# MoE layer of a small vision tower: the first expert matrix is copied into fixed buffers before use

## Chip, core and metric

The kernel is one program on one core of a Trainium2 chip. Its time is the device time of that core in microseconds (us), as the median of several runs. Five engines work side by side and meet at semaphores: TensorE (PE, matmuls; PEld is its weight load), VectorE (DVE), ScalarE (ACT), GpSimd (POOL) and SyncE (SP, which here only issues DMAs). SBUF is the on-chip memory of 128 partitions; a DMA is carried out by up to 16 DMA engines.

## What is computed

Patches of 32 images (1,152 tokens of width 192) are embedded, pass three steps of a reference attention with layernorms, a softmax attention and then a mixture of experts (MoE). Only the MoE part changes:

```python
logits = xn @ gate_w                                   # 8 experts
top_logits, top_idx = jax.lax.top_k(logits, 2)
top_gates = softmax(top_logits)
h = gelu(einsum('td,edh->teh', xn, w1) + b1)           # w1[e]: 192 x 768
y = einsum('teh,ehd->ted', h, w2) + b2                 # w2[e]: 768 x 192
out = sum over the two chosen experts of gate * y
```

## The kernel before

**Data.** Each token's row is scattered twice by POOL's indirect DMAs into `srt_dram`, sorted by expert and padded so that each expert starts at a tile of 128 rows. There are always 25 tiles (`NTILE`). Which expert a tile belongs to is known only at run time: DVE computes it (`exp_ready`, numbers packed in `packs`) and where its rows start (`row_i`, `place_ready`). Every weight is held twice in SBUF, as a float16 high part and a bfloat16 low part (`w1h`, `w1l`, `w2h`, `w2l`, all 8 experts), which ACT and POOL make from float32 pieces during the attention steps (SP loads a piece of `w1` as 96 x 768, ahead of its turn).

**One tile, i.** SP reads the tile's start from `row_i` and loads 128 x 194 values from `srt_dram` into a ring of eight (`xsrt`, shown as `xT` in the profile, since it lies in that tensor). PE transposes it (`columns_of`, `srtT`), ACT applies the layernorm gain (`srtT_affine`), DVE rounds it to `xh`, POOL takes the rest `xl`. `first(i)` is 12 groups of three matmuls (six blocks of 128 hidden units, two halves of 96 input features, each high x high, high x low, low x high), with the expert's weights as the stationary operand; their address depends on the expert, so each group has register instructions. ACT adds the bias and applies gelu, one instruction for each of the six blocks of 128 x 128. DVE splits the result (`split`), and `second(i)` is 18 matmuls of 192 columns against `w2`. DVE adds `b2`, POOL scatters the rows to `y_dram`.

**Order.** Everything is written out by hand, engine by engine. On PE the order is `columns_of(i+1)`, `first(i)`, `second(i-1)`. SP, in its own queue, waits for `place_ready` and `row_stored` and then issues the 25 row loads; the one for tile i waits until ring slot i-8 is free. After the last tile SP loads `y_dram` back in tiles of 108 tokens (`yab`, the last one 72), PE sums, and a last layernorm stores the output.

Of the kernel before, what the change touches and what calls it, by code (L numbers as in the profile page):

```python
# [5 lines left out]
ALU = mybir.AluOpType  # L6
# [35 lines left out]
RING, YB = 8, 3  # L42
PACK = 7
# [14 lines left out]
def vit_kernel(nc, d, out):  # L58
    with ExitStack() as ctx:
# [13 lines left out]
        vecs = sb("vecs", [T, 5, C])  # L73
# [13 lines left out]
        wqk = sb("wqkh", [HF, 2, 2, 384], F16), sb("wqkl", [HF, 2, 2, 384], BF16)  # L87
# [3 lines left out]
        w1h, w1l = sb("w1h", [HF, EXP, 2, HID], F16), sb("w1l", [HF, EXP, 2, HID], BF16)  # L91
        w2h, w2l = sb("w2h", [P, EXP, HJ, C], F16), sb("w2l", [P, EXP, HJ, C], BF16)
        b1 = sb("b1", [128, EXP, HJ])
# [13 lines left out]
        e1T = sb("e1T", [E1, NTOK])  # L107
# [104 lines left out]
        xh, xl = sb("xh", [HF, 2, 2, P], F16), sb("xl", [HF, 2, 2, P], BF16)  # L212
# [13 lines left out]
        x_in = [sem(f"x_in{t}") for t in range(NT)]  # L226
# [3 lines left out]
        ffn_in = sem("ffn_in")  # L230
        piece_in = [sem(f"piece_in{b}") for b in range(4)]
        srt_in = [sem(f"srt_in{b}") for b in range(RING)]
        y_stored = [sem(f"y_stored{b}") for b in range(YB)]
        yab_in = [sem(f"yab_in{t}") for t in range(NT)]
# [28 lines left out]

        def expert_of(engine, loaded, i):

            if i % PACK == 0:
                loaded[0] = engine.value_load(packs[0:1, i // PACK:i // PACK + 1], min_val=0, max_val=EXP ** PACK - 1)
            return (loaded[0] >> 3 * (i % PACK)) & EXP - 1

        def weights(q, low):  # L270

            if q < 2:
                return wqk[low][:, q].rearrange("p k c -> p (k c)"), stage[q % 4][0:HF, 0:4 * C]
            if q == 2:
                return wvp[low][:].rearrange("p a k c -> p (a k c)"), stage[q % 4][0:HF, 0:4 * C]
            e, k = (q - 3) // 3, q % 3
            if k < 2:
                return (w1h, w1l)[low][:, e, k, :], stage[q % 4][0:HF, 0:HID]
            return (w2h, w2l)[low][:, e].rearrange("p j c -> p (j c)"), stage[q % 4]
# [3 lines left out]
        FFN = ["vbb", "qkbm", "gate", "b1", "route", "rank"]  # L283
        tiles = dict(gains=gains, vbb=vbb, vecs=vecs, fc1=fc1, fc1b=fc1b, fc2=fc2, fc2b=fc2b, ident=ident, sel=sel, rowm=rowm,
                     kw=kw, wqT=wqT, bdm=bdm, wq=wq, wqv=wqv, pairm=pairm, wpa=wpa,
                     qkbm=qkbm, gate=gate, b1=b1, route=route, rank=rank)

        @block.sync
        def _(sp):
            sp.dma_start(tokw[:], d["tokw"]).then_inc(tokw_in, 16)  # L290
            for t in range(2):
                sp.dma_start(xT[:, t], d["xT"][t]).then_inc(x_in[t], 16)
            for name in EARLY:
                sp.dma_start(tiles[name][:], d[name]).then_inc(early_in, 16)
            for t in range(2, NT):
                sp.dma_start(xT[:, t], d["xT"][t]).then_inc(x_in[t], 16)
# [6 lines left out]
            for i in range(NI + 1):  # L303
                if i < NI:
                    sp.wait_ge(S["o_ready"], i + 1)
                    for j in range(JB):
                        sp.dma_start(scratch[i % SCR].rearrange("(j h n d) -> j n h d", j=JB, h=HEADS, n=N)[j],
                                     osb[j * N:(j + 1) * N, i % OB, j].rearrange("p (h d) -> p h d", h=HEADS)
                                     ).then_inc(o_stored[i % 2], 16)
                if 1 <= i <= NI:  # L310
                    q = i - 1
                    sp.wait_ge(o_stored[q % 2], 16 * JB * (q // 2 + 1))
                    if q >= 4:
                        sp.wait_ge(S["ocT_psum"], q - 3)
                    sp.dma_start(oc[:, q % 4], scratch[q % SCR].rearrange("(p c) -> p c", p=T)).then_inc(oc_loaded[q % 4], 16)

                for q in range(PIECES):
                    if (turn_of(q - 4) if q >= 4 else 0) != i:
                        continue
                    if q == 2:  # L320
                        sp.wait_ge(S["e1_psum"], len(CHUNKS))
                        sp.wait_ge(S["k_psum"], 4)
                    if q >= 4:
                        sp.wait_ge(S["low_ready"], q - 3)
                    e, k = q // 3 - 1, q % 3
                    if e < 0:
# [15 lines left out]
            for b in range(YB):  # L342
                sp.wait_ge(y_stored[b], 16 * len(range(b, NTILE, YB)))
            for t in range(NT):
                n = T if t < NT - 1 else LAST
                sp.dma_start(yab[0:n, t].rearrange("p k c -> p (k c)"),
                             y_dram[2 * t * T:2 * (t * T + n)].rearrange("(p k) c -> p (k c)", k=2)).then_inc(yab_in[t], 16)
# [8 lines left out]
        def _(pe):  # L356
# [23 lines left out]
            for t in range(NT + 1):  # L380
                if t == 1:
                    pe.wait_ge(early_in, 16 * len(EARLY))
                if t < NT:
                    pe.wait_ge(x_in[t], 16)
# [141 lines left out]
            for i in range(NT + 6):  # L526
                if i < NT:
# [6 lines left out]
                    for a in range(2):  # L534
                        for g in range(3):
                            cols = slice(g * 128, (g + 1) * 128)
                            last = split_mm(bank[5 + a][:, g * T:(g + 1) * T], [(wqk[0][:, a, k, cols], wqk[1][:, a, k, cols]) for k in range(2)], x)
# [86 lines left out]
            def first(i, e):  # L624

                pe.wait_ge(S["xh_ready"], i + 1)
                pe.wait_ge(S["xl_ready"], i + 1)
                for j in range(HJ):
                    if j % 2 == 0 and hid_turn(i, j) >= 4:
                        pe.wait_ge(S["hid_ready"], 2 * (hid_turn(i, j) - 3))  # L630
# [26 lines left out]
            for i in range(NTILE + 1):  # L657
                if i + 1 < NTILE:
                    columns_of(i + 1)
                if i < NTILE:  # L660
                    e[i % 2] = expert_of(pe, loaded, i)
                    first(i, e[i % 2])
# [9 lines left out]
            pe.wait_ge(S["hid_ready"], HJ * NTILE)  # L672
# [5 lines left out]
            for t in range(NT):  # L678
                n = T if t < NT - 1 else LAST
                pe.wait_ge(yab_in[t], 16)  # L680
# [8 lines left out]
        def _(act):  # L689
# [155 lines left out]
            act.wait_ge(S["exp_ready"], 1)  # L845
            loaded = [None]
            for i in range(NTILE):
                if i + 1 < NTILE:
                    srtT_affine(i + 1)
                e = expert_of(act, loaded, i)  # L850
# [16 lines left out]
        def _(dve):  # L867
# [30 lines left out]
            V.memset(ocT[HF:], 0.0).then_inc(S["pad_ready"], 1)  # L898
            link(V.memset(exp_f[:], 0.0))
# [255 lines left out]
            def sorted_high(i):  # L1155
                dve.wait_ge(S["srtT_ready"], i + 1)
                V.tensor_copy(xh[:, i % 2], x32[:, i % 2]).then_inc(S["xh_ready"], 1)  # L1157

            def split(i):
                for a in range(2):  # L1160
                    cols = slice(a * 3 * P, (a + 1) * 3 * P)
                    o = slice(a * 3, (a + 1) * 3)
                    dve.wait_ge(S["hid_ready"], HJ * i + 3 * (a + 1))
# [38 lines left out]
        def _(pool):  # L1202
# [32 lines left out]
            for i in range(3, NI + 6):  # L1235
                if 5 <= i < NI + 5:
# [15 lines left out]
            for i in range(NT + 6):  # L1252
                if 0 <= i - 4 < NT:
# [24 lines left out]
            def sorted_low(i):  # L1278
# [3 lines left out]
                G.tensor_tensor(xl[:, i % 2], x32[:, i % 2], xh[:, i % 2], ALU.subtract).then_inc(S["xl_ready"], 1)  # L1282
# [97 lines left out]
```

## Time and profile before

| | us |
|---|---|
| median of 3 runs (547.84 to 556.38) | 551.46 |
| the profiled execution: its own time | 549.04 |
| the profiled execution: span from first to last instruction | 547.2 |
| PE busy in it | 445.6 |
| DVE / ACT / POOL busy | 318.5 / 237.0 / 220.9 |
| DMA queue q1 (issued by SP), share of 16 engines | 19.1% |

Busy time is a sum over the span. PE is busy for four fifths of it. The granted TensorE clock averages 0.813 of full speed. "DMA share" in later rows is the busy share of the 16 DMA engines together, so a share of 1 is all 16 at work.

### The profile page before, as it was taken

How to read it: one execution, taken by the hardware profiler on the slowest of the kernel's cores; microseconds unless marked ns; L12 is line 12 of the kernel's file. 1: busy time of each engine (PE TensorE's matmuls, PEld its weight loads, DVE VectorE, ACT ScalarE, POOL GpSimd, SP SyncE). 2: the span in 40 equal slices, each digit the busy share in tenths (PEclk: the TensorE clock that was granted, in tenths of full speed). 3: DMA queues.
4: the chain of work that ended last, by engine and by line, in shares of the span. 5: the costliest groups of instructions: out<-in, count | busy, mean ns of one | idle time of the engine just before them, and what ended most of it. 6: DMA issues, size and time to landing. Idle time of an engine off the chain costs nothing.

```text
span 547.2 us, 13333 instructions
## 1 busy us (share of the span) xinstructions
PE 445.6 (81%) x4370; PEld 352.7 (64%) x4370; DVE 318.5 (58%) x912; ACT 237.0 (43%) x687; POOL 220.9 (40%) x334
## 2 busy tenths in 40 slices
PE   3992588799999965489999998763299999999975
PEld 3972545466666544389898897663287677676764
DVE  1110323388888888687878877545466556565523
ACT  0130324365555532277666654401265554555403
POOL 1000003345545547545446744355334534445214
PEclk9996587799999995567667867555589999999988
DMA  8609513454545541000000000002211111110023
GB/s 265 221 11 323 192 45 74 120 126 108 118 116 122 110 104 18 2 1 3 1 4 14 13 15 14 13 25 85 65 45 46 42 26 41 28 31 21 11 75 121
DMA packets 52161, 38.46 MB, mean 70 GB/s; under 512 B 36187, under 2 KB 45541, under 8 KB 51328
## 3 DMA queue, kind: packets, MB, share of 16 engines
q1 hardware_dynamic: 48832, 26.89, 19.1%
q10 hardware_dynamic: 1008, 7.15, 4.0%
q0 software_dynamic: 2256, 3.57, 2.0%
q8 instruction: 39, 0.64, 0.5%
q14 instruction: 26, 0.21, 0.1%
HBM read 24.00 MB, written 14.33 MB: 70 GB/s over the span
## 4 chain that ended last, share of the span: by engine, by line
PE 61%; DVE 12%; issue 9%; POOL 6%; DMA 4%; ACT 3%; ACTq 3%; SPq 2%; POOLq 0%; DVEq 0%
PE wide L358 29%; PE bank L358 25%; PE bank L363 3%; ACTq L706 3%; PE bank L545 2%; POOL rstd L1222 2%; DVE xs L895 2%; ACT xT L801 2%; POOL srt_dram L1249 1%; PE bank L621 1%; DMA bdm<-in_bdm 1%; DVE rm L985 1%; PE wide L545 1%; DVE xT L993 1%; DMA xT<-in_w 1%
## 5 line engine op out<-in xcount | busy, mean ns | idle before, releaser
L1295 POOL DMA_INDIRECT y_dram<-qkbm,ydst x25 | 25.8, 1032 | 70.7 <-PE bank L358 27.3
L691 ACT ACTIVATE xT<-wide 108x384 f32<-108x384 f32 (+1 forms) x70 | 26.0, 407 | 60.1 <-PE wide L358 44.9
L895 DVE TENSOR_SCALAR xs<-yb,mv,rstd 108x192 f32<-108x192 f32 x24 | 43.5, 1814 | 5.4 <-POOL rstd L1222 5.0
L358 PE MATMUL bank<-xT 108*32 108x96 f32 (+4 forms) x629 | 32.3, 265 | 16.5 <-ACT xT L691 10.7
L358 PEld LDWEIGHTS bank<-xT 108*32 108x32 f32 (+4 forms) x629 | 24.1, 143 | 33.2 <-issue 21.3
L724 ACT ACTIVATE xT<-bank,gains 96x128 f32<-96x128 f32 (+1 forms) x72 | 28.7, 454 | 38.4 <-PE bank L621 31.9
L358 PE MATMUL bank<-wqv,xTs 128*108 128x384 f32 x96 | 41.0, 554 | 3.4 <-DVE xT L993 3.4
L1167 DVE CAST xs<-xT 128x384 f16<-128x384 f32 x50 | 21.6, 431 | 35.7 <-ACT xT L855 34.7
L358 PE MATMUL wide<-w2h,xs 128*128 x300 | 41.9, 248 | 0.4
L1249 POOL DMA_INDIRECT srt_dram<-row,dst x22 | 22.8, 1037 | 42.0 <-DVE dst L1050 34.0
L1221 POOL TENSOR_SCALAR veps<-mv 108x1 f32<-108x1 f32 x46 | 10.7, 232 | 70.8 <-DVE mv L889 70.2
L358 PE MATMUL wide<-xT,wqkh 96*128 96x108 f16 (+1 forms) x264 | 35.1, 287 | 3.3 <-DVE xT L1014 3.3
L358 PE MATMUL bank<-xh,w1h 96*128 96x128 f16 x152 | 35.4, 234 | 2.5 <-DVE xh L1157 1.3
L1244 POOL TENSOR_TENSOR wqkl<-xT,wqkh 96x768 bf16<-96x768 f32 x2 | 3.2, 1634 | 83.9 <-ACT wqkh L691 83.9
L358 PE MATMUL wide<-w2l,xs 128*128 x150 | 37.0, 246 | 0.0
L358 PE MATMUL wide<-xT 108*108 108x17 f16 (+4 forms) x511 | 36.7, 217 | 0.0
L358 PE MATMUL wide<-xh,w1h 96*128 96x128 f16 x148 | 33.9, 232 | 1.4 <-issue 1.1
L801 ACT ACTIVATE xT<-bank,nmax 108x108 f32<-108x108 f32 x99 | 25.1, 368 | 22.5 <-DVE nmax L1060 22.5
L358 PEld LDWEIGHTS wide<-xT 108*108 108x108 f16 (+4 forms) x511 | 34.6, 151 | 0.0
L358 PE MATMUL bank<-xl,w1h 96*128 96x128 bf16 x152 | 34.2, 227 | 0.0
L358 PE MATMUL wide<-xT,wqkl 96*128 96x108 f16 x132 | 34.2, 287 | 0.0
L358 PE MATMUL bank<-xh,w1l 96*128 96x128 f16 x152 | 34.1, 225 | 0.0
(230 smaller groups left out, 1283.1 us busy)
## 6 DMA issues: line engine op xcount, KB each, us to landing
srt_dram<-row ACTq DMA_DIRECT2D x8, 800.2 KB, 10.4
xT<-in_xT SPq DMA_DIRECT2D x11, 324.0 KB, 6.6
xT<-srt_dram SPq DMA_DIRECT2D x25, 97.0 KB, 2.0
hT<-in_w SPq DMA_DIRECT2D x8, 288.0 KB, 3.2
xT<-in_w SPq DMA_DIRECT2D x8, 288.0 KB, 3.2
xT<-in_w SPq DMA_DIRECT2D x4, 576.0 KB, 4.0
hT<-in_w SPq DMA_DIRECT2D x4, 576.0 KB, 3.8
scratch<-xT SPq DMA_DIRECT2D x72, 27.0 KB
```

Of the source, the lines that this page charges most:

```text
L358: return nc.tensor.matmul(o, l, r, start=start, stop=stop)
L363: last = nc.tensor.transpose(o[:, f, :], i[:, f * HF:(f + 1) * HF], ident[0:T, 0:T])
L545: last = nc.tensor.transpose(bank[1 + r][0:T, g * T:(g + 1) * T], prob[:, 3 * r + g, :], ident[0:T, 0:T])
L691: return nc.scalar.activation(o, i, ACT.Copy)
L706: nc.scalar.dma_start(srt_dram[z * 96:(z + n) * 96].rearrange("(p r) w -> p (r w)", p=96), blank[:, 0:n * W]).then_inc(S["zeroed"], 16)
L724: last = nc.scalar.activation(o[:, f], i[:, f], ACT.Identity, scale=gains[:, which, 0, f:f + 1], bias=gains[:, which, 1, f:f + 1])
L801: last = nc.scalar.activation(prob[:, hh, :], bank[1 + r][0:T, g * T:(g + 1) * T], ACT.Exp, bias=nmax[:, hh:hh + 1])
L895: return V.tensor_scalar(o, x, mv[0:rows, n % 4, 0:1], r[0:rows, n % 4:n % 4 + 1], ALU.subtract, ALU.mult)
L1167: V.tensor_copy(high, hidf[:, i % 2, cols]).then_inc(S["hidh_ready"], 1)
L1222: last = G.tensor_tensor(rstd[0:rows, k], ve, nhalf[0:rows], ALU.pow)
L1249: G.indirect_dma_start(srt_dram, bass.IndirectOffsetOnAxis(dst[:, t, k:k + 1], 0), row[:, t, 0:W], None, bounds_check=EXP * CAP - 1, oob_i ...
L1295: G.indirect_dma_start(y_dram, bass.IndirectOffsetOnAxis(ydst[:, q:q + 1], 0), ysb[:, q % YB], None, bounds_check=2 * NTOK - 1, oob_is_err ...
```

## The change

- Three fixed buffers (`w1s`, `WB = 3`), laid into tensors that are free by then (`tokw` and `e1T`, `vecs` and `wqv`, `wqkh` and `wqkl`), hold the high and low `w1` of one tile's expert. SP reads the expert number and copies 97 partitions x 1,536 values of 2 bytes for each part, two DMAs for every tile, SBUF to SBUF. The first three tiles' copies are issued ahead of the first row load; the copy for tile i waits until `first(i-3)` is finished. Row loads of tiles 3 to 24 and copies now alternate in SP's queue.
- `first` takes the weights from constant addresses, on all 128 partitions. Partition 96 of `w1` holds `b1`, partition 96 of `xh` holds ones, and the partitions above are zero. The `w1` pieces are loaded as 128 x 768 instead of 96 x 768.
- ACT applies gelu to 128 x 256 at a time (three instructions for a tile), without a bias operand and without reading the expert number.
- The zeros and ones are written by eight new memsets, six on DVE and two on POOL (`tokw`, and `vecs` in the softmax attention's second turn).

```diff
+        w1s = [(slot_at(tokw[:].rearrange("p k c -> p (k c)"), F16), slot_at(e1T_all[:], BF16)),
+               (slot_at(vecs_all[:].rearrange("p v c -> p (v c)"), F16), slot_at(wqv[:].rearrange("p k c -> p (k c)"), BF16)),
+               (wqk[0][:].rearrange("p a k c -> p a (k c)"), wqk[1][:].rearrange("p a k c -> p a (k c)"))]
...
             sp.wait_ge(S["lg_psum"], NT)
             sp.dma_start(b2, d["b2"]).then_inc(S["b2_in"], 16)
-            sp.wait_ge(S["place_ready"], 1)
-            sp.wait_ge(S["row_stored"], 16 * 2 * NT)
-            for i in range(NTILE):
+            def expert_weights(i):
+
+                e = expert_of(sp, loaded, i)
+                if i >= WB:
+                    sp.wait_ge(S["hid_psum"], HJ // 2 * (i - WB + 1))
+                for o, w in zip(w1s[i % WB], (w1h, w1l)):
+                    sp.dma_start(o[0:HF + 1], w[0:HF + 1, bass.ds(e, 1)].rearrange("p a k n -> p (a k) n")).then_inc(w1_in[i % WB], 16)
+
+            def sorted_rows(i):
...
+            loaded = [None]
+            sp.wait_ge(S["rows_ready"], 1)
+            sp.wait_ge(S["exp_ready"], 1)
+            for i in range(WB):
+                expert_weights(i)
+            sp.wait_ge(S["place_ready"], 1)
+            sp.wait_ge(S["row_stored"], 16 * 2 * NT)
+            for i in range(WB):
+                sorted_rows(i)
+            for i in range(WB, NTILE):
+                sorted_rows(i)
+                expert_weights(i)
...
-            def first(i, e):
+            def first(i):
 
                 pe.wait_ge(S["xh_ready"], i + 1)
                 pe.wait_ge(S["xl_ready"], i + 1)
+                pe.wait_ge(w1_in[i % WB], 32 * (i // WB + 1))
...
-                        high, low = (w[:, bass.ds(e, 1), k, j * P:(j + 1) * P].rearrange("p a n -> p (a n)") for w in (w1h, w1l))
+                        high, low = (w[:, k, j * P:(j + 1) * P] for w in w1s[i % WB])
...
-                for j in range(HJ):
+                for j in range(0, HJ, 2):
                     act.wait_ge(S["hid_psum"], hid_turn(i, j) + 1)
                     if i >= 2 and j == 0:
                         act.wait_ge(S["hidl_ready"], 2 * (i - 1))
-                    nc.scalar.activation(hidf[:, i % 2, j * P:(j + 1) * P], hid_block(i, j), ACT.Gelu,
-                                         bias=b1[:, bass.ds(e, 1), j]).then_inc(S["hid_ready"], 1)
+                    nc.scalar.activation(hidf[:, i % 2, j * P:(j + 2) * P], hid_pair(i, j), ACT.Gelu).then_inc(S["hid_ready"], 1)
...
+                if i == 1:
+                    pool.wait_ge(S["fb_ready"], 1)
+                    pool.wait_ge(S["qkl_ready"], 2)
+                    G.memset(w1s[1][0][HF:], 0.0).then_inc(S["rows_ready"], 1)
+                    pool.wait_ge(S["rows_ready"], 1)
```

On PE, the start of one tile's `first` before (ISA and REGISTER_ALU rows compute an address):

```order
L358 REGISTER_ALU [waits hid_ready,xl_ready,xh_ready]
L358 REGISTER_ALU
L358 ISA
L358 MATMUL bank<-xh,w1h 128x128
L358 MATMUL bank<-xl,w1h 128x128
L358 REGISTER_ALU
L358 MATMUL bank<-xh,w1l 128x128
L358 ISA
```

and in the changed kernel, for a tile that uses the buffer in `tokw` and `e1T`:

```order
L390 MATMUL bank<-xh,tokw 128x128 [waits w1_in0,hid_ready,xl_ready,xh_ready]
L390 MATMUL bank<-xl,tokw 128x128
L390 MATMUL bank<-xh,e1T 128x128
L390 MATMUL bank<-xh,tokw 128x128
L390 MATMUL bank<-xl,tokw 128x128
L390 MATMUL bank<-xh,e1T 128x128
```

The two register rows in each group are gone, and a wait for the copy (`w1_in0`) stands at the head of the tile.

On SP, the queue after the load of `b2` before:

```order
L333 DMA hT<-in_b 128x1536 [waits lg_psum]
L337 TENSOR_LOAD row_i [waits row_stored,place_ready]
L337 ISA x2
L341 ISA
L341 DMA xT<-srt_dram 128x194
```

and in the changed kernel, with the first tile's two copies (two more pairs follow before the first row load):

```order
L346 DMA hT<-in_b 128x1536 [waits lg_psum]
L280 TENSOR_LOAD packs [waits exp_ready,rows_ready]
L280 ISA x2
L353 REGISTER_ALU
L353 ISA
L353 DMA tokw<-w1h 97x1536
L353 REGISTER_ALU
L353 DMA e1T<-w1l 97x1536
```

Six copies of 97 x 1,536 values now stand ahead of the first load of sorted rows.

## Rows read from the trace of the kernel before

**Rows 1.** The page, part 1: busy us (share of the span) xinstructions.
```profile
PE 445.6 (81%) x4370; PEld 352.7 (64%) x4370; DVE 318.5 (58%) x912; ACT 237.0 (43%) x687; POOL 220.9 (40%) x334
```
**Rows 2.** Windows: us; busy of each engine (instructions); clock, DMA share, GB/s.
```profile
380.00:394.00 14.00, 2.14 (x9) 1.25 (x9) 7.93 (x37) 1.81 (x5) 4.61 (x5) 0.50 0.28 87
...
439.00:449.00 10.00, 9.96 (x112) 7.13 (x111) 5.64 (x17) 5.46 (x16) 4.75 (x6) 1.00 0.13 34
...
469.00:479.00 10.00, 9.93 (x112) 7.10 (x110) 5.56 (x16) 5.45 (x16) 4.09 (x6) 1.00 0.09 19
```
**Rows 3.** Timeline of PE, full clock: start us, duration, instruction.
```profile
440.08 0.23 PE L358 MATMUL wide<-xh,w1h 96*128 96x128 f16 x1
440.15 0.22 PE L358 MATMUL wide<-xl,w1h 96*128 96x128 bf16 x1
440.20 0.22 PE L358 MATMUL wide<-xh,w1l 96*128 96x128 f16 x1
440.32 0.23 PE L358 MATMUL bank<-xh,w1h 96*128 96x128 f16 x1
```
**Rows 4.** Timeline of PE, first tile, half clock.
```profile
394.62 0.31 PE L358 MATMUL bank<-xh,w1h 96*128 96x128 f16 x1
394.73 0.31 PE L358 MATMUL bank<-xl,w1h 96*128 96x128 bf16 x1
394.84 0.31 PE L358 MATMUL bank<-xh,w1l 96*128 96x128 f16 x1
394.94 0.31 PE L358 MATMUL bank<-xh,w1h 96*128 96x128 f16 x1
```
**Rows 5.** Timeline of all engines, start of the expert tiles.
```profile
385.12 0.16 DVE L1140 CAST packs<-pack_f 1x4 int32<-1x4 f32 x1
...
386.18 0.17 DVE L1143 SCALAR_TENSOR_TENSOR row_i<-route,of 1x25 int32<-1x25 f32 x1
...
388.82 8.46 SPq L341 DMA_DIRECT2D xT<-srt_dram  x8
...
391.03 0.64 PE L621 MATMUL bank<-ident,xT 128*96 128x128 f32 x2 [10.17 <-DMA xT<-srt_dram]
...
393.99 0.29 PE L358 MATMUL bank<-xh,w1h 96*128 96x128 f16 x1 [1.34 <-DVE xh L1157]
```
**Rows 6.** Windows, three stretches with much DMA (columns as in rows 2).
```profile
14.00:20.00 6.00, 6.00 (x38) 5.82 (x37) 0.72 (x2) 0.69 (x2) 0.00 (x0) 0.91 1.05 385
41.00:54.00 13.00, 3.90 (x33) 3.55 (x31) 1.30 (x3) 0.00 (x0) 0.00 (x0) 0.68 1.00 322
...
534.00:535.00 1.00, 1.00 (x8) 1.00 (x7) 0.58 (x3) 0.00 (x0) 0.79 (x2) 1.00 0.79 273
535.00:536.00 1.00, 1.00 (x9) 1.00 (x8) 0.85 (x3) 0.12 (x1) 0.61 (x3) 1.00 0.77 286
```
**Rows 7.** Timeline of SP's DMA issues after the last tile.
```profile
528.04 4.47 SPq L346 DMA_DIRECT2D xT<-y_dram  x11
536.42 4.56 SPq L352 DMA_DIRECT2D out<-xT  x6
```
**Rows 8.** The page's DMA issues: count, KB each, median us from issue to landing.
```profile
srt_dram<-row ACTq DMA_DIRECT2D x8, 800.2 KB, 10.4
xT<-in_xT SPq DMA_DIRECT2D x11, 324.0 KB, 6.6
xT<-srt_dram SPq DMA_DIRECT2D x25, 97.0 KB, 2.0
hT<-in_w SPq DMA_DIRECT2D x8, 288.0 KB, 3.2
...
xT<-in_w SPq DMA_DIRECT2D x4, 576.0 KB, 4.0
hT<-in_w SPq DMA_DIRECT2D x4, 576.0 KB, 3.8
```
**Rows 9.** Timeline of PE, start of the last tile's first layer.
```profile
517.87 0.23 PE L358 MATMUL bank<-xh,w1h 96*128 96x128 f16 x1
```
**Rows 10.** Timeline of POOL and DVE at the start: memsets and the work behind.
```profile
0.73 1.89 POOL L1233 MEMSET row<- 108x2145 f32 x1 [0.29 <-POOLq L1370]
...
0.89 0.42 DVE L897 MEMSET xTs<- 32x432 f32 x1 [0.89 <-PEq L1370]
...
12.06 0.36 DVE L907 TENSOR_TENSOR h<-bank,vecs 108x192 f32<-108x192 f32 x1 [9.79 <-DMA bdm<-in_bdm]
```

More of the change, by code:

```diff
@@ L42 @@
 RING, YB = 8, 3
+WB = 3
 PACK = 7
@@ L72, in vit_kernel @@
         tokw = sb("tokw", [128, KF, C])
-        vecs = sb("vecs", [T, 5, C])
+        vecs_all = sb("vecs", [P, 5, C])
+        vecs = vecs_all[0:T]
         gains = sb("gains", [HF, 3, 2, 2])
@@ L90, in vit_kernel @@
         gate = sb("gate", [HF, 2, EXP])
-        w1h, w1l = sb("w1h", [HF, EXP, 2, HID], F16), sb("w1l", [HF, EXP, 2, HID], BF16)
+        w1h, w1l = sb("w1h", [P, EXP, 2, HID], F16), sb("w1l", [P, EXP, 2, HID], BF16)
         w2h, w2l = sb("w2h", [P, EXP, HJ, C], F16), sb("w2l", [P, EXP, HJ, C], BF16)
-        b1 = sb("b1", [128, EXP, HJ])
         ident = sb("ident", [P, P])
@@ L106, in vit_kernel @@
         hT = hT_all[0:HF]
-        e1T = sb("e1T", [E1, NTOK])
+        e1T_all = sb("e1T", [P, NTOK])
+        e1T = e1T_all[0:E1]
         ex = sb("ex", [T, NT, E2])
@@ L211, in vit_kernel, with slot_at @@
         rsa = sb("rsa", [T, 3, NT])
-        xh, xl = sb("xh", [HF, 2, 2, P], F16), sb("xl", [HF, 2, 2, P], BF16)
+        xh, xl = sb("xh", [P, 2, 2, P], F16), sb("xl", [P, 2, 2, P], BF16)
+        def slot_at(place, dt):
+            return place[:, 0:HID].bitcast(dt).rearrange("p (k n) -> p k n", k=2)
+        w1s = [(slot_at(tokw[:].rearrange("p k c -> p (k c)"), F16), slot_at(e1T_all[:], BF16)),
+               (slot_at(vecs_all[:].rearrange("p v c -> p (v c)"), F16), slot_at(wqv[:].rearrange("p k c -> p (k c)"), BF16)),
+               (wqk[0][:].rearrange("p a k c -> p a (k c)"), wqk[1][:].rearrange("p a k c -> p a (k c)"))]
         parts = xs_all[:].rearrange("p t c -> p (t c)")
@@ L223, in vit_kernel @@
         scratch = nc.dram_tensor("scratch", [SCR, JB * HEADS * N * HD], F32, kind="Internal").ap()
-        x_in = [sem(f"x_in{t}") for t in range(NT)]
+        tile_in = [sem(f"tile_in{t}") for t in range(NT)]
         tokw_in = sem("tokw_in")
@@ L230, in vit_kernel @@
         ffn_in = sem("ffn_in")
+        w1_in = [sem(f"w1_in{b}") for b in range(WB)]
         piece_in = [sem(f"piece_in{b}") for b in range(4)]
@@ L233, in vit_kernel @@
         y_stored = [sem(f"y_stored{b}") for b in range(YB)]
-        yab_in = [sem(f"yab_in{t}") for t in range(NT)]
         o_stored = [sem(f"o_stored{i}") for i in range(2)]
@@ L262, in hid_block, with hid_pair @@
             return bank[2 + hid_turn(i, j) % 4][:, (j % 2) * P:(j % 2 + 1) * P]
+        def hid_pair(i, j):
+            return bank[2 + hid_turn(i, j) % 4][:, 0:2 * P]
         def expert_of(engine, loaded, i):
@@ L272, in weights @@
             if q < 2:
-                return wqk[low][:, q].rearrange("p k c -> p (k c)"), stage[q % 4][0:HF, 0:4 * C]
+                return wqk[low][0:HF, q].rearrange("p k c -> p (k c)"), stage[q % 4][0:HF, 0:4 * C]
             if q == 2:
@@ L277, in weights @@
             if k < 2:
-                return (w1h, w1l)[low][:, e, k, :], stage[q % 4][0:HF, 0:HID]
+                return (w1h, w1l)[low][:, e, k, :], stage[q % 4][:, 0:HID]
             return (w2h, w2l)[low][:, e].rearrange("p j c -> p (j c)"), stage[q % 4]
@@ L291, in _ @@
             for t in range(2):
-                sp.dma_start(xT[:, t], d["xT"][t]).then_inc(x_in[t], 16)
+                sp.dma_start(xT[:, t], d["xT"][t]).then_inc(tile_in[t], 16)
             for name in EARLY:
@@ L295, in _ @@
             for t in range(2, NT):
-                sp.dma_start(xT[:, t], d["xT"][t]).then_inc(x_in[t], 16)
+                sp.dma_start(xT[:, t], d["xT"][t]).then_inc(tile_in[t], 16)
             for name in DIFF:
@@ L346, in _ @@
                 sp.dma_start(yab[0:n, t].rearrange("p k c -> p (k c)"),
-                             y_dram[2 * t * T:2 * (t * T + n)].rearrange("(p k) c -> p (k c)", k=2)).then_inc(yab_in[t], 16)
+                             y_dram[2 * t * T:2 * (t * T + n)].rearrange("(p k) c -> p (k c)", k=2)).then_inc(tile_in[t], 16)
             out_tiles = out.rearrange("b n c -> (b n) c")
@@ L383, in _ @@
                 if t < NT:
-                    pe.wait_ge(x_in[t], 16)
+                    pe.wait_ge(tile_in[t], 16)
                     if t >= 2:
@@ L536, in _ @@
                             cols = slice(g * 128, (g + 1) * 128)
-                            last = split_mm(bank[5 + a][:, g * T:(g + 1) * T], [(wqk[0][:, a, k, cols], wqk[1][:, a, k, cols]) for k in range(2)], x)
+                            last = split_mm(bank[5 + a][:, g * T:(g + 1) * T], [(wqk[0][0:HF, a, k, cols], wqk[1][0:HF, a, k, cols]) for k in range(2)], x)
                         last.then_inc(S["qk_psum"], 1)
@@ L661, in _ @@
                     e[i % 2] = expert_of(pe, loaded, i)
-                    first(i, e[i % 2])
+                    first(i)
                 if i >= 1:
@@ L671, in _ @@
             pe.wait_ge(S["srtT_ready"], NTILE)
-            pe.wait_ge(S["hid_ready"], HJ * NTILE)
+            pe.wait_ge(S["hid_ready"], HJ // 2 * NTILE)
             for t in range(8):
@@ L679, in _ @@
                 n = T if t < NT - 1 else LAST
-                pe.wait_ge(yab_in[t], 16)
+                pe.wait_ge(tile_in[t], 32)
                 if t >= 8:
@@ L898, in _ @@
             V.memset(ocT[HF:], 0.0).then_inc(S["pad_ready"], 1)
+            for o in (w1s[0][1], *w1s[2], xl):
+                V.memset(o[HF:], 0.0)
+            link(V.memset(xh[HF:], 0.0))
+            link(V.memset(xh[HF:HF + 1, :, 0], 1.0))
             link(V.memset(exp_f[:], 0.0))
@@ L1156, in sorted_high @@
                 dve.wait_ge(S["srtT_ready"], i + 1)
[L1157 removed]
+                V.tensor_copy(xh[0:HF, i % 2], x32[:, i % 2]).then_inc(S["xh_ready"], 1)
             def split(i):
@@ L1162, in split @@
                     o = slice(a * 3, (a + 1) * 3)
-                    dve.wait_ge(S["hid_ready"], HJ * i + 3 * (a + 1))
+                    dve.wait_ge(S["hid_ready"], HJ // 2 * i + 2 + a)
                     if i >= 2 and a == 0:
@@ L1235, in _ @@
             for i in range(3, NI + 6):
+                if i == 4:
+                    pool.wait_ge(S["tok_psum"], NT)
+                    link(G.memset(w1s[0][0][HF:], 0.0))
                 if 5 <= i < NI + 5:
@@ L1345 @@
     route[:, 96:96 + PACK] = float(EXP) ** np.arange(PACK)
+    w1 = np.zeros((EXP, P, 2, HID), np.float32)
+    w1[:, :HF] = a["ffn_w1"].reshape(EXP, 2, HF, HID).transpose(0, 2, 1, 3)
+    w1[:, HF, 0] = a["ffn_b1"]
     data = {
@@ L1360 @@
         "gate": halves(a["ffn_gate_w"]),
-        "w1": a["ffn_w1"].reshape(EXP, 2, HF, HID).transpose(0, 2, 1, 3),
+        "w1": w1,
         "w2": a["ffn_w2"].reshape(EXP, HJ, 128, C).transpose(0, 2, 1, 3),
-        "b1": a["ffn_b1"].reshape(EXP, HJ, 128).transpose(2, 0, 1), "b2": np.broadcast_to(a["ffn_b2"][None], (P, EXP, C)),
+        "b2": np.broadcast_to(a["ffn_b2"][None], (P, EXP, C)),
         "ident": np.eye(P), "sel": sel,
```

17 lines of the change are left out of this document (7 added, 10 removed).

## The prediction

> **What bounds the kernel now.** I read the page's busy times first: PE is busy for 445.6 us of 547.2, far ahead of the rest [rows 1]. Then windows of 10 us along the stretch that the change is about, the 25 expert tiles. There PE is busy 9.9 to 10 us of 10 at the full clock (2.4 GHz), the other engines for about half or less, and the DMA engines for 9 to 14% [rows 2]. So this stretch is bound by what PE issues, and DMA has room, if all 16 engines share the work. Its first layer starts at 393.99 and that of the last tile at 517.87 [rows 5, 9]: 123.9 us for 24 tiles, 5.16 us a tile. After it 29.3 us are left to the end of the span.
>
> Then the timeline of PE inside a tile. Three matmuls of 128 columns stand 0.07 and 0.05 us apart, then 0.12 us pass before the next group [rows 3]. In the long gap stand the register instructions that the change removes. At the half clock all gaps are 0.10 to 0.11 us [rows 4]; there the registers cost nothing.
>
> **What the change removes.** A group takes 0.24 us; without its long gap it would be about 0.18. That is 0.06 x 12 groups = 0.7 us a tile, about 17 us over 24 tiles at the full clock. ACT goes from six instructions to three in a tile; ACT is about half busy [rows 2], so this buys nothing. All this counts only while PE is what each tile waits for.
>
> **What it adds, and the choice on which everything hangs.** Each tile now waits for two copies of 97 partitions x 3,072 bytes = 298 KB each, 596 KB a tile, 50 copies in all. Are they spread over 16 DMA engines? Look at transfers by their number of partitions. With 128 and 96 partitions the DMA share reaches 1.05 and 1.00 [rows 6, 8]. From 528 to 532.5 SP issues only the loads of `y_dram`, 108 partitions each (the last 72), and then nothing until 536.42 [rows 7]. In that flow the share stays at 0.77 to 0.79 [rows 6]. Set against the 1.05 of a saturated stretch, 0.79 is 0.75 of 16: 12 engines. If rows were dealt out in portions rounded up, 7 to an engine, 108 rows would occupy all 16. Twelve engines means nine whole rows for each: the row count is cut into equal shares, by a number that divides it. For 97, a prime, that number is 1. I take this: **each copy runs on one DMA engine**, and both of a tile on the same one, since nothing in the two differs that would send them apart.
>
> The Trainium skill (DMA: Bandwidth & Descriptors, "Why a DMA increments its semaphore by 16 and not by 1") says it outright: the largest number up to 16 that divides the slowest dimension of both sides, and on SP's queue the lowest-numbered engines. By that rule 108 gives 12, where the trace agrees, and 97 gives engine 0 alone, which no row of the kernel before shows.
>
> **The price of one copy.** The rate of one engine: 385 GB/s on 16 is 24.1 [rows 6]; 286 on 12 is 23.8. Stores of blanks to DRAM give 322 on 16, 20.1. From landing times, 288 KB more costs 0.6 to 0.8 us [rows 8], 18.4 KB per engine in that time, 23 to 31 GB/s. No row shows SBUF to SBUF, nor one engine alone. Ends: 31 GB/s is 9.7 us a copy, 20.1 is 14.8 us. I take 25 GB/s, 11.9 us, next to the saturated loads and a little above, since one engine alone contends with nobody.
>
> The same skill page ("Specifications") gives an engine about 27 GiB/s, 29 GB/s; by that a copy would be an estimated 10.3 us and the whole 80 us shorter than my sum.
>
> **The sum**, along that one engine:
> - Start. `packs` is ready at 385.3 [rows 5]. SP reads it (1.2 us, about the spacing of its row loads: eight issued and landed in 8.46 us) and the first byte moves some 1.2 us after the issue. First packet at 387.7.
> - Three pairs of copies back to back, 3 x 23.8 = 71.4: 459.1. SP's first row loads stand behind them in the same engine's ring (8 of their 128 rows each). In the kernel before they were issued at 388.82 and landed by 391.03; now they land at about 460.
> - A hole. The fourth pair waits for `first(0)`. From landing to the first matmul 3.0 us [rows 5], 36 matmuls at 0.107, since PE has long been idle and is at the half clock [rows 4], 3.9 us, then SP's wake-up and first byte, 1.8. The engine starts again at 468.7.
> - 22 more tiles. The third buffer keeps work queued on the engine, so it doesn't pause. A tile costs 23.8 plus that engine's part of row load, scatter and instruction fetch: 14% of 5.16 us = 0.7 [rows 2]. 22 x 24.5 = 539: 1007.7, landed 1008.7.
> - The end. 29.3 us from the last first layer as before, plus 3 for the half clock: 1 in `first(24)` (3.9 against 2.9), at most 2.8 in two second layers (18 x 0.16 against 1.5 each), cut off as the clock rises. 1041.
> - Edits at nearly nothing: six DVE memsets of 32 partitions at 0.2 to 0.8 us each (432 values took 0.42) lie before DVE's first work at 12.06 [rows 10]. POOL's two, 1.4 us each by its 2,145 values in 1.89: the one on `tokw` falls where POOL has little to do, the one on `vecs` stands ahead of its work in the softmax attention and costs 0 to 1.4 us; I take 1. The `w1` pieces are a third longer, 16 loads of 96 KB more, over 100 us in which DMA is half busy: 0 to 1 us.
>
> The span comes to 1042; the profiled execution's own time was 1.8 us above its span, 549.04 against 547.2. That is **1044 us**. The median of the runs shown, 551.46, is 2.4 above the profiled one, which is noise beside this. In the trace of the kernel before, nothing waits for the resource that is now full: one ring of SP's queue.
>
> **Rivals.**
> - *The copies spread, and it is faster.* The mechanism: equal shares hold for loads from DRAM, but an SBUF-to-SBUF copy is dealt out over 14 to 16 engines. Then 596 KB take 1.5 to 1.8 us of a tile and hide behind PE; PE's 17 us come in. The start pays: six issues at about 0.45 us and 1.8 MB ahead of the first rows, 2 us. 549.0 - 17 + 2 = 534 us. It decides if the copies' engines number five or more, where both fit in 4.5 us. For it: no such copy is in the trace. Against: 108 partitions used 12. Chance 0.08.
> - *They spread, and PE gains nothing*, because the register gap hides another limit on pairs of weight load and matmul. The mean in a group is 0.08 us a matmul already [rows 3]; if that were a floor, the time is 549 + 2 = 551. Against it: two of three gaps are 0.05 and 0.07. Chance 0.03. The Trainium skill (TensorE: Matmul & The Clock Gate, "Back-to-back issue gap") states just such a sustained 81 ns for N=128; the rows' single gaps of 0.05 speak against it as a floor.
> - *One engine for each copy, but two different ones for a tile's pair.* The pairs run side by side: the sum's copy time halves, 1044 - 25 x 11.9 = 746 us. Chance 0.05.
> - *One engine for both*: 0.84.
>
> **The numbers.** Predicted 1044. The range takes in most of the price's bounds: at 9.7 us a copy the time is 1044 - 50 x 2.2 = 934; at 13.6 us it is 1129. The slow end of 14.8 (1189) is that of stores to DRAM, the row least like a copy inside SBUF, and I leave the last part out. With 0.16 for the rivals outside, 930 to 1130 leaves out about 2 in 10. Two per cent is about what a measurement of this kernel can tell. Faster by more: 0.08. Within: 0.03. Slower: 0.89.
>
> **What would show it.** PE's gaps in a group should be even, but in short bursts of some 4 us at the half clock, every 24 us. PE's idle time should end with the DMAs from `w1h` and `w1l`; DMA share in the tile stretch should be 1/16 and a little, 0.06 to 0.12, at some 25 GB/s; the first matmul of `first(0)` should come near 463, seventy us later than before. ACT, DVE and POOL keep their durations. The prediction is wrong if the share in that stretch is 0.3 or more, or if the first row load lands before 400.

## The result, and the profile after

The changed kernel takes 1033.11 us (median of 4 runs, 1028.17 to 1034.01) against 550.57 before: a ratio of 1.878 (95% interval 1.867 to 1.888). Predicted were 1044, range 930 to 1130. The profiled execution took 1034.01, its span is 1032.2.

The page of the changed kernel, parts 1 and 2 (busy tenths in 40 slices of 25.8 us):

```profile
PE 461.7 (45%) x4370; PEld 392.6 (38%) x4370; DVE 314.7 (30%) x918; ACT 218.5 (21%) x612; POOL 221.2 (21%) x336
...
PE   6858899757999730004222222222222222223335
...
DMA  8353555500000010010000000000000000000003
```

PE's sum barely moved [rows 1], but from slice 20 on it is busy a fifth of the time, and the DMA digit is 0 until the last slice. No engine looks busy there. Windows of that stretch (columns as in rows 2):

```profile
394.00:450.00 56.00, 0.00 (x0) 0.00 (x0) 0.00 (x0) 0.00 (x0) 0.00 (x0) 0.50 0.07 27
...
500.00:600.00 100.00, 23.86 (x238) 22.11 (x235) 12.51 (x35) 7.86 (x21) 10.02 (x13) 0.66 0.09 33
600.00:700.00 100.00, 21.72 (x224) 20.53 (x224) 10.97 (x32) 7.81 (x20) 8.97 (x12) 0.65 0.09 33
```

For 56 us no engine does anything. A DMA share of 0.07 is 1.1 of 16 engines, and they move 27 GB/s: one DMA engine at full rate looks like an idle machine in a mean over 16. The windows of [rows 2] had shares of 0.09 and 0.13 while the tiles ran at full speed; this stretch has no more, and is full.

SP's queue in the changed kernel (start us, duration of the issue, what it issues):

```profile
386.52 0.80 SPq L353 DMA_DIRECT2D tokw<-w1h  x1
387.46 1.93 SPq L353 DMA_DIRECT2D e1T<-w1l  x1
389.71 8.14 SPq L353 DMA_DIRECT2D vecs<-w1h  x1
397.97 15.82 SPq L353 DMA_DIRECT2D wqv<-w1l  x1
414.09 11.38 SPq L353 DMA_DIRECT2D wqkh<-w1h  x1
425.63 11.30 SPq L353 DMA_DIRECT2D wqkl<-w1l  x1
438.61 13.87 SPq L360 DMA_DIRECT2D xT<-srt_dram  x4
467.80 0.72 SPq L353 DMA_DIRECT2D tokw<-w1h  x1
```

The first row load, issued at 388.82 before [rows 5], is issued at 438.61. From the third copy on an issue takes 8 to 16 us: SP is held inside the instruction. The first rows have landed by 460.8, where PE's timeline begins again; here are its start and, from the second tile, the spacing at the full clock:

```profile
460.79 1.06 PE L653 MATMUL bank<-ident,xT 128*96 128x128 f32 x4 [79.87 <-DMA xT<-srt_dram]
463.51 0.27 PE L390 MATMUL bank<-xh,tokw 128*128 128x128 f16 x1 [1.66 <-POOL xl L1323]
...
469.00 0.22 PE L390 MATMUL bank<-xh,wqv 128*128 128x128 f16 x1
469.06 0.22 PE L390 MATMUL bank<-xh,vecs 128*128 128x128 f16 x1
469.12 0.22 PE L390 MATMUL bank<-xl,vecs 128*128 128x128 bf16 x1
469.17 0.22 PE L390 MATMUL bank<-xh,wqv 128*128 128x128 f16 x1
```

The gap of 0.12 us of [rows 3] is gone: 0.055 throughout, 0.167 us a group instead of 0.24. The change does what it says on PE. It is not what the tiles wait for. From the waits, and from the chain of work that ended last:

```profile
PE bank L653 <- DMA xT<-srt_dram: 460.0, 22, 79.9
```
```profile
965.75 34.11 DMA e1T<-w1l
```

PE waits 460 us for row loads, and the last copy, issued at 965.75, lands 34.11 us later, at 999.9. That the waits name the row loads and not the copies follows from the order of work: PE transposes the rows of tile i+1 before it starts `first(i)`, and the load of those rows stands in SP's queue behind the copies for tile i. When those rows are there, the copies for tile i have just landed.

The packets of the copies (rows of 3,072 bytes) can be counted in the same trace. In 575 of the 591 us in which any is under way it is exactly one; two overlap in the other 16. The next starts 0.120 us after the last (median). Copies on two engines would run side by side, since several stand in the queue at once; so all stand on one.

### The profile page after: what moved, and what is told of

Read it like the earlier page. It is cut to its first block, busy times and chain, and to the rows that moved or that the text cites. A ratio compares the mean times of both kernels' runs of the same rounds, so it can differ in the third digit from the quotient of the medians.

```text
span 1032.2 us, 12640 instructions
## 1 busy us (share of the span) xinstructions
PE 461.7 (45%) x4370; PEld 392.6 (38%) x4370; DVE 314.7 (30%) x918; ACT 218.5 (21%) x612; POOL 221.2 (21%) x336
## 4 chain that ended last, share of the span: by engine, by line
SPq 53%; PE 21%; DMA 8%; DVE 6%; issue 6%; POOL 3%; ACT 2%; ACTq 1%; POOLq 0%; DVEq 0%
SPq L353 28%; SPq L360 22%; PE bank L390 10%; PE wide L390 8%; DMA e1T<-w1l 3%; DMA xT<-srt_dram 2%; SPq L356 2%; PE bank L395 2%; ACTq L739 1%; ACT xT L834 1%; PE bank L577 1%; DVE xs L924 1%; POOL rstd L1255 1%; DMA bdm<-in_bdm 1%; ACT xT L724 1%
## 5 line engine op out<-in xcount | busy, mean ns | idle before, releaser
L653 PE MATMUL bank<-ident,xT 128*96 128x128 f32 x50 | 16.0, 427 | 460.0 <-DMA xT<-srt_dram 460.0
L653 PEld LDWEIGHTS bank<-ident,xT 128*96 128x96 f32 x50 | 6.1, 174 | 464.9 <-DMA xT<-srt_dram 384.9
L1190 DVE CAST xh<-xT 96x256 f16<-96x256 f32 x25 | 7.5, 300 | 471.2 <-ACT xT L757 471.2
L1323 POOL TENSOR_TENSOR xl<-xT,xh 96x256 bf16<-96x256 f32 x25 | 16.7, 668 | 448.4 <-DVE xh L1190 448.4
L390 PE MATMUL wide<-w2h,xs 128*128 x300 | 44.1, 264 | 0.0
L924 DVE TENSOR_SCALAR xs<-yb,mv,rstd 108x192 f32<-108x192 f32 x24 | 41.1, 1713 | 5.7 <-POOL rstd L1255 5.3
L1200 DVE CAST xs<-xT 128x384 f16<-128x384 f32 x50 | 18.5, 370 | 59.9 <-ACT xT L885 59.7
L390 PE MATMUL bank<-tokw,xT 128*108 128x192 f32 x132 | 27.8, 368 | 8.9 <-DMA xT<-in_xT 5.4
L390 PEld LDWEIGHTS wide<-xT,wqkh 96*128 96x128 f16 x264 | 29.2, 138 | 3.6 <-issue 3.5
L390 PEld LDWEIGHTS wide<-w2h,xs 128*128 128x128 f16 (+1 forms) x300 | 29.6, 108 | 0.4
## 6 DMA issues: line engine op xcount, KB each, us to landing
srt_dram<-row ACTq DMA_DIRECT2D x8, 800.2 KB, 10.3
```

The lines of the kernel that those rows point to most:

```text
L390: return nc.tensor.matmul(o, l, r, start=start, stop=stop)
L653: last = nc.tensor.transpose(srtT(i % 2)[:, f, :], xsrt[:, i % RING, f * HF:(f + 1) * HF], ident[:])
L924: return V.tensor_scalar(o, x, mv[0:rows, n % 4, 0:1], r[0:rows, n % 4:n % 4 + 1], ALU.subtract, ALU.mult)
L1200: V.tensor_copy(high, hidf[:, i % 2, cols]).then_inc(S["hidh_ready"], 1)
```

## The experiments

Ratios are to the kernel before on the same chip, with their 95% intervals.

**The row count alone.** Three kernels change only how many rows each copy takes (rows above 96 of `w1h` and `w1l` hold zeros, so they can be copied):

```diff
-                    sp.dma_start(o[0:HF + 1], w[0:HF + 1, bass.ds(e, 1)]...
+                    sp.dma_start(o[:], w[:, bass.ds(e, 1)]...              # 128 rows
+                    sp.dma_start(o[0:HF + 2], w[0:HF + 2, bass.ds(e, 1)]... # 98 rows
+                    sp.dma_start(o[0:106], w[0:106, bass.ds(e, 1)]...      # 106 rows
```

> The changed kernel with the copies of w1 on 128 partitions instead of 97 (31 rows of zeros more, a third more bytes). My theory, that the row count sets the number of DMA engines in equal shares: 128 rows use 16 engines, 8 rows of 3,072 bytes each, at 0.122 us a row about 1 us a copy; the copies hide, PE bounds the tiles again. A tile falls from 5.16 to about 4.2 us (a group of three matmuls 0.167 instead of 0.24 us, as the changed kernel's trace shows), the start pays 2 us: 525 to 532 us, ratio to before 0.96. Rival, that copies inside SBUF are slow by their bytes or by their kind: 390 KB a copy instead of 298, 1200 us. Rival, that the register gap hid another limit: 550 us.

> The changed kernel with one row more in each copy, 98 instead of 97, 1% more bytes. My theory: 98 = 14 x 7, so 14 engines, 7 rows each, 0.85 us a copy: 525 to 533 us, the same as with 128 rows within 0.5%. Rival, that only multiples of 16 are spread: about 1035 us. Rival, that the size or kind of copy costs: about 1040 us.

> The changed kernel with copies of 106 rows, which is 2 x 53. My theory, the largest divisor up to 16: two engines, 53 rows of 0.122 us = 6.5 us a copy, 13 us and 0.7 for the other traffic a tile: 387.5 + 39 + 10 + 22 x 13.7 + 30 = 768 us. Rival, that any row count but a prime is spread well: 530 us. Rival, that a ragged count falls back to one engine: 9% above the changed kernel, about 1085 us.

Measured:

| rows in a copy | its largest divisor up to 16 | us, median | ratio (95%) |
|---|---|---|---|
| 97 | 1 | 1033.11 | 1.878 (1.867 to 1.888) |
| 106 | 2 | 769.81 | 1.404 (1.393 to 1.414) |
| 98 | 14 | 536.74 | 0.977 (0.970 to 0.984) |
| 128 | 16 | 521.92 | 0.951 (0.945 to 0.957) |

One row more, 1% more bytes, takes 496 us away. That is neither bytes nor kind of copy. 106 rows come within 2 us of the 768 worked out for two engines. A count that is not a multiple of 16 is spread (98). The traces show the engine counts themselves: of the copies' packets exactly two are under way in 300 of 332 us with 106 rows, and the most frequent number is 14 with 98 rows and 16 with 128. By the Trainium skill (DMA: Bandwidth & Descriptors, "Why a DMA increments its semaphore by 16 and not by 1") the number is the largest divisor up to 16; the runs agree at 97 and 106, while at 98 the time is no longer set by the engines. With 98 rows I had expected the 128-row time within 0.5%; it is 15 us above. That miss has its own experiments below.

**Both copies of a pair on one engine?** The high part stays at 97 rows, the low part gets 128:

```diff
-                for o, w in zip(w1s[i % WB], (w1h, w1l)):
-                    sp.dma_start(o[0:HF + 1], w[0:HF + 1, bass.ds(e, 1)]...
+                for o, w, n in zip(w1s[i % WB], (w1h, w1l), (HF + 1, P)):
+                    sp.dma_start(o[0:n], w[0:n, bass.ds(e, 1)]...
```

> The changed kernel with the high part still copied on 97 rows and the low part on 128. My theory, that both parts' 97-row copies stand on the same DMA engine: that engine now has 11.9 us for the high part, 1 us of the low part and 0.7 of other traffic a tile, 13.6: about 768 us. Rival, that the two copies of a pair ran on two engines or that SP's issue held them: it stays near 1030 us.

770.41 us (ratio 1.400, 1.392 to 1.409). Curing one of two halves the excess, so the two had been one after the other. Had they run side by side on two engines, each would have needed the 24 us of a tile by itself, and the one left uncured would have kept them. The saving is (1033.1 - 770.4) / 25 = 10.5 us a tile, near the 11.9 of a copy less the 1 us that 128 rows still cost.

**What PE gains, and from what.** First with no copies and a constant address, which leaves out the choice of the expert, then with no copies and register addresses, the rest of the change kept:

```diff
-                        high, low = (w[:, bass.ds(e, 1), k, j * P:(j + 1) * P]...  # kernel before
+                        high, low = (w[:, 0, k, j * P:(j + 1) * P] for w in (w1h, w1l))
```

> The kernel before, with the first layer always reading expert 0's w1 from a constant address (which expert it reads is left out of the computation), no copies, gelu as before. It prices the register instructions on PE alone. My theory: 12 groups a tile fall from 0.24 to 0.167 us and the pauses for instruction fetch get rarer, a tile goes from 5.16 to about 4.2 us: 549 - 23 = 526 us, ratio 0.955 to 0.96. Rival, that ACT with six gelu instructions and two affine (3.1 us a tile) or the chain over POOL holds the tile: 4.8 us or more a tile, 540 us or more.

```diff
-                        high, low = (w[:, k, j * P:(j + 1) * P] for w in w1s[i % WB])   # changed kernel
+                        high, low = (w[:, bass.ds(e, 1), k, j * P:(j + 1) * P]... for w in (w1h, w1l))
```

> The changed kernel without its copies: first layer on 128 rows with the bias row and gelu on 256 columns, but the weights read in place by register addresses as before. My theory, that constant addresses on PE are the only gain: 549 us, within 1% of before. Rival, that ACT's shorter work (1.1 us a tile less) or the rows 96 to 127 move the time: 540 or less, or 555 or more.

521.12 us (ratio 0.949, 0.943 to 0.955) and 548.47 us (0.995, 0.991 to 0.999). Constant addresses alone give the whole gain; the bias row and the wider gelu alone give 0.5%, by the interval 0.1 to 0.9%. Windows of the same 70 us, in the kernel before, with a fixed expert, with 128-row copies and with 98-row copies:

```profile
410.00:480.00 70.00, 68.14 (x747) 48.91 (x745) 40.45 (x107) 36.11 (x108) 32.37 (x42) 1.00 0.14 38
```
```profile
410.00:480.00 70.00, 67.87 (x986) 64.07 (x984) 60.16 (x142) 45.83 (x142) 46.24 (x53) 1.00 0.15 42
```
```profile
410.00:480.00 70.00, 67.64 (x989) 64.25 (x987) 60.39 (x142) 34.09 (x89) 46.01 (x53) 1.00 0.70 248
```
```profile
410.00:480.00 70.00, 61.35 (x869) 58.45 (x867) 50.21 (x124) 28.68 (x77) 40.66 (x48) 0.98 0.59 177
```

PE issues 747 matmuls before and 986 to 989 without register instructions, at nearly the same busy time: a busy PE was not a full one. That is 5.2 us a tile against 3.95. Of these 1.2 us the twelve groups give 12 x 0.073 = 0.9; the other 0.3 lies in longer pauses. What makes those pauses was not tested. The copies raise the DMA share from 0.15 to 0.70 and cost the tiles nothing. With 98 rows 869 matmuls get through, and PE idles.

**The gelu merge**, undone in the 128-row kernel:

```diff
-                    nc.scalar.activation(hidf[:, i % 2, j * P:(j + 2) * P], hid_pair(i, j), ACT.Gelu).then_inc(S["hid_ready"], 1)
+                    for h2 in range(2):
+                        last = nc.scalar.activation(hidf[:, i % 2, (j + h2) * P:(j + h2 + 1) * P], hid_block(i, j + h2), ACT.Gelu)
+                    last.then_inc(S["hid_ready"], 1)
```

> The kernel with copies of 128 rows, with gelu again on 128 columns, six instructions a tile instead of three. Work on ACT goes from about 2.1 to 3.1 us a tile, below PE's 3.95. My theory: no change, 522 us within 1%. Rival, that the gelu merge is part of the gain: 526 us or more.

526.6 us, ratio 0.963 (0.956 to 0.971) against 0.951 (0.945 to 0.957), on another chip. That is within the 1% that my theory allowed and also the rival's 526, so the time decides nothing: the ratios differ by 1.3 points and their intervals touch. In the same 70 us PE issues 971 matmuls instead of 989, 2% of the tile stretch, about 2 us or 0.4% of the whole. The fixed-expert kernel has 986 with six gelus, which speaks for less. What the merge is worth stays open, between nothing and a little over 1%. The work that it saves ACT is less than I had expected: the six instructions took 273 ns each here (median), not 367 as in the kernel before, where they had a bias operand.

**Why 98 rows are slower than 128.** In the trace of the 98-row kernel PE waits for row loads 22.2 us in nine places between 394 and 495. One of them, 16.2 us, is the wait for the first rows, which takes 14.5 us with 128 rows too; the other 6 us lie in eight places inside the tile stretch. SP's queue there, one tile after another:

```profile
448.31 0.35 SPq L360 DMA_DIRECT2D xT<-srt_dram  x1
449.04 0.89 SPq L353 DMA_DIRECT2D vecs<-w1h  x1
450.05 0.80 SPq L353 DMA_DIRECT2D wqv<-w1l  x1
452.97 0.33 SPq L360 DMA_DIRECT2D xT<-srt_dram  x1
```

and in the 128-row kernel:

```profile
447.26 0.35 SPq L360 DMA_DIRECT2D xT<-srt_dram  x1
448.66 0.50 SPq L353 DMA_DIRECT2D vecs<-w1h  x1
449.27 0.53 SPq L353 DMA_DIRECT2D wqv<-w1l  x1
451.17 0.35 SPq L360 DMA_DIRECT2D xT<-srt_dram  x1
```

An issue takes 0.89 and 0.80 us on 14 engines, 0.50 and 0.53 on 16, and the value load ahead of the next row load takes longer too (median 1.3 us against 0.75). From one row load to the next SP takes 4.6 us on average (3.9 in the 128-row kernel); PE needs 3.95. To tell a full queue from a bad order, row loads were issued four tiles ahead, for both row counts, with one pair of copies ahead of the first rows:

```diff
+            for i in range(WB, WB + 4):
+                sorted_rows(i)
             for i in range(WB, NTILE):
-                sorted_rows(i)
+                if i + 4 < NTILE:
+                    sorted_rows(i + 4)
                 expert_weights(i)
```

> Copies of 98 rows (14 engines), one pair ahead of the first rows, and the row loads issued four tiles ahead of the copies that they stood beside. The first 98-row kernel took 4.45 us a tile against 3.96 with 128 rows, and PE waited for row loads in nine tiles. Theory A, SP's own queue is the limit (a copy on 14 engines costs it 0.89 and 0.80 us to issue, on 16 engines 0.50 and 0.53, about 4.1 to 4.4 us a tile in all): loading rows earlier doesn't cure it, the copies are then late instead, 4.2 us or more a tile, 524 us or more. Theory B, only the order is at fault, rows issued too late behind the copies: 3.96 us a tile, 518 us as with 128 rows.

> The fastest version so far (copies of 128 rows, one pair ahead of the first rows) with row loads four tiles earlier. With 128 rows PE hardly waits for rows (PE busy 9.7 us of 10), so my theory says no change, 517 us within 0.5%. Rival, that a late row load still costs pauses in some tiles: 514 us or less.

536.4 us (0.980, 0.973 to 0.987) and 519.39 us (0.946, 0.941 to 0.951), the second within the 0.5% expected. Earlier rows cure nothing at 98 rows; PE now waits for the copies instead, as theory A says. In the timeline of PE of that kernel:

```profile
437.30 0.22 PE L395 MATMUL wide<-xh,tokw 128*128 128x128 f16 x1 [1.43 <-DMA e1T<-w1l]
441.84 0.22 PE L395 MATMUL wide<-xh,vecs 128*128 128x128 f16 x1 [0.67 <-DMA wqv<-w1l]
```

The obvious mend of 97, 96 rows and the bias row by itself, meets the same limit:

```diff
-                    sp.dma_start(o[0:HF + 1], w[0:HF + 1, bass.ds(e, 1)]...
+                    for rows in (slice(0, HF), slice(HF, HF + 1)):
+                        sp.dma_start(o[rows], w[rows, bass.ds(e, 1)]...
```

> The changed kernel with each 97-row copy cut in two: 96 rows, and the bias row by itself; four DMAs a tile instead of two. My theory: 96 rows use 16 engines, 6 rows each, and one row on one engine is 0.1 us, so the slow engine is gone. What is late next is SP's own queue: in the 128-row kernel it needs 3.1 to 3.4 us a tile when nothing holds it, two more issues of 0.5 to 0.8 us each make it 4.2 to 5 us, above PE's 3.95: 528 to 545 us, and like the 98-row kernel it should wait for row loads. Rival, that SP is not a limit: 522 us as with 128 rows. Rival, that the 97-row slowness has another cause than the row count of one DMA: 1030 us.

542.19 us (0.990, 0.980 to 0.999). The slow engine is gone, as expected. But SP now has four issues a tile of 0.53 to 0.56 us (median) in place of two, takes 4.7 us from one row load to the next, and nearly all of PE's gain is lost with that.

**The start of the tiles.**

```diff
-            for i in range(WB):
-                expert_weights(i)
+            expert_weights(0)
             sp.wait_ge(S["place_ready"], 1)
             sp.wait_ge(S["row_stored"], 16 * 2 * NT)
-            for i in range(WB):
-                sorted_rows(i)
+            sorted_rows(0)
+            sorted_rows(1)
+            expert_weights(1)
+            sorted_rows(2)
+            expert_weights(2)
```

> The kernel with copies of 128 rows, but on SP only the first tile's pair of copies stands ahead of the first two row loads; the pairs of tiles 1 and 2 follow them. In the 128-row kernel the first matmul of the tiles came 12.7 us after packs, in the kernel before 8.7. My theory, that the six copies (six issues and 2.4 MB) ahead of the first rows delay the start: 3 to 4 us less, 518 us, about 0.7% faster than with six ahead. Rival, that the start is held by the scattered rows or by the POOL and ACT chain: no change, 522 us.

> As the kernel with only the first pair ahead, and copies of 112 rows instead of 128: 16 engines, 7 rows each, 12% fewer bytes. My theory: PE bounds the tiles, bytes on 16 engines don't matter: the same as with 128 rows within 0.5%. Rival, that the 0.7 DMA share of the 128-row kernel delays row loads or scatters: 2 to 4 us faster than with 128.

517.28 us (0.937, 0.932 to 0.942) and 518.88 us (0.943, 0.939 to 0.947). `packs` (DVE) and the first matmul of the tiles, with six copies ahead of the rows:

```profile
381.82 0.16 DVE L1173 CAST packs<-pack_f 1x4 int32<-1x4 f32 x1
394.72 0.26 PE L390 MATMUL bank<-xh,tokw 128*128 128x128 f16 x1 [1.10 <-POOL xl L1323]
```

and with two ahead, in the kernel with 112 rows:

```profile
381.34 0.16 DVE L1175 CAST packs<-pack_f 1x4 int32<-1x4 f32 x1
390.54 0.27 PE L392 MATMUL bank<-xh,tokw 128*128 128x128 f16 x1 [1.07 <-POOL xl L1325]
```

From 12.9 to 9.2 us, measured from start to start: 3.7 us, as expected (with 128 rows and earlier row loads it is 8.6 us). 112 rows are no faster than 128. In the times the three quickest kernels with this start (0.937, 0.943, 0.946) lie below the one without (0.951), but only the first one's interval is clear of it; the gain is seen in the trace, its size in the median is not settled between 0.5 and 1.4%. The best version stands at 517 us, 6% below the kernel before.

## Why the prediction was right

Its mechanism, one DMA engine for all copies, held, and the times of its sum nearly so:

| step of the sum | predicted | trace |
|---|---|---|
| first copy issued | 386.5 | 386.52 |
| first rows landed | 460 | 460.8 |
| first matmul of the tiles | 463 | 463.51 |
| fourth pair under way | 468.7 | issued 467.80 |
| a tile after that | 24.5 | (999.9 - 467.8) / 22 = 24.2 |
| last copy landed | 1008.7 | 999.9 |
| from there to the end of the span | 32.3 | 32.3 |

- *The engine count* was the step on which all hung. It was read from 0.79 against 1.05 of a DMA share in a stretch with only 108-row transfers [rows 6, 7]. The times with 97 and 106 rows and the packets with 98 and 128 confirm it.
- *The price of a copy*, 11.9 us, was taken between 9.7 and 14.8. Six copies from 386.5 to 460.8, less 2 us of latency, give 12.0; by the packets' own spacing, 0.121 us in a run without interruption, a copy is 97 x 0.121 = 11.7. That the choice came within 2% is partly luck: no row had a copy inside SBUF or an engine alone, and the rows allowed some 20% either way. The rate by engine of the Trainium skill (DMA: Bandwidth & Descriptors, "Specifications"), from which 10.3 us came as an estimate, is too fast for rows of 3,072 bytes here.
- *A tile* took 24.2 us and not 24.5; over 22 tiles that makes most of the 9 us by which I overshot. The two terms share it. By the packets two copies were 23.5 us, not 23.8, and the other traffic on that engine was about 0.6 us, 0.28 of it the row load, where I had 0.7 from the DMA share before.
- *The rivals.* The spread copies never ran with 97 rows, but what they would have given was priced at 534; the 128-row kernel shows 522. The 17 us for PE's gain were too few: 1.2 us in each of 24 tiles is 29, since a group lost 0.07 us and not 0.06, and the longer pauses got rarer too. The condition of that rival was also off by one: with five engines two copies take 23.8 / 5 = 4.8 us, more than the 4.5 of a tile, so it needed six. The rival of a floor of 0.08 us a matmul is dead: 0.056 was sustained over the 36 matmuls of a first layer, 2.0 us for the layer, so the 81 ns of the Trainium skill (TensorE: Matmul & The Clock Gate, "Back-to-back issue gap") is no floor for these shapes.
- *The six copies ahead of the rows* I priced at 2 us if spread; they cost 3.7 more than two ahead.
- *Named as a sign, and half wrong:* bursts at the half clock. The granted clock in the stretch averages 0.57 to 0.66, not 0.5. In the first tiles it can be seen to rise: the spacing goes from 0.107 to 0.056 us at 468.8, after PE had worked without a break since 463.5.
- *Named as a sign, and wrong:* that PE's idle time should end with the copies. Only one wait of 17.8 us, for the last tile, ends with a copy (`e1T<-w1l`); 460 us end with row loads. I had overlooked that PE takes the next tile's rows before it uses this tile's weights. The price is the same, since the rows wait behind the copies.
- I expected the row loads to be issued on time and to wait in the engine's ring, its list of transfers to be done. In fact SP was held for 50 us in issuing the copies. The sum is the same, since the engine had to finish the copies first either way, but any other DMA on SP's queue would have been late too.

## What to carry to other kernels

Choose the partition count of a DMA so that a large number up to 16 divides it. Here 96, 112 and 128 rows were spread over all engines and 97 put everything on one; padding with zeros cost far less than one odd row. Before moving addresses out of a compute engine, count what the moving queue pays for each issue: here SP had 3.95 us a tile, and a row load with two copies on 16 engines just fitted, while two copies on 14 engines or four on 16 did not. In a profile, look twice at a DMA share near 1/16 beside idle engines: here it was one saturated DMA engine, not spare bandwidth.

## What the runs showed of the hardware

- Three pairs of weight load and matmul (96 or 128 rows, 128 columns) with register-computed addresses took 0.24 us at the full clock, with constant ones 0.167; at the half clock both take 0.32. That the register instructions cost time only where the matmuls are short enough is how I read this.
- An issue of a copy on SP takes longer on 14 engines (0.80 to 0.89 us with 98 rows) than on 16 (0.50 to 0.53 with 128 rows, 0.55 with 112), with fewer bytes. Why was not tested. On one engine with much work queued an issue takes nearly as long as a copy, 10.5 us.
- Gelu on 128 x 128 took 367 ns with a bias operand at a computed address (kernel before) and 273 without (merge undone); on 128 x 256 without it took 383 (128-row kernel). Each line has min/median/max in ns:

```profile
L855 ACT ACTIVATE xT<-bank,b x76: 358/367/376, 397.0 to 520.4; 128x128 f32<-128x128 f32 x76
```
```profile
L886 ACT ACTIVATE xT<-bank x76: 261/273/278, 396.3 to 493.2; 128x128 f32<-128x128 f32 x76
```
```profile
L885 ACT ACTIVATE xT<-bank x38: 368/383/384, 396.2 to 491.6; 128x256 f32<-128x256 f32 x38
```

  So the merged instruction is hardly longer than one of those that it replaces only because it lost its bias as well: 128 columns more cost 110 ns. In a tile the six instructions of before take 2.2 us, six without bias 1.6, three merged ones 1.1.
- One DMA engine copying 3,072-byte rows inside SBUF sustained 0.121 us a row, 25 GB/s.
